# A mixture-of-experts layer whose first 17 expert tiles are formed from three of four images, and the rest from what is left

## The chip, the cores and the metric

One core of one Trainium2 chip. The metric is device time in microseconds (us), the median of the runs shown. Engine names: PE is TensorE (matmul), DVE is VectorE, ACT is ScalarE, POOL is GpSimd, SP is SyncE, which issues DMAs. PEld is TensorE's weight load.

## What is computed

The input is 4 images of 1024 tokens with 256 channels. Three blocks follow one another: a convolution-style attention, a multi-head attention with 8 heads, and a mixture of experts. The change is in the last:

```python
xt = layernorm(t).reshape(-1, 256)                  # 4096 tokens
route_prob = softmax(xt @ Wr + br)                  # 8 experts
routes = argmax(route_prob, axis=-1)
for e in range(8):
    h = gelu(xt @ W1[e] + b1[e])                    # 256 -> 1024
    y = h @ W2[e] + b2[e]                           # 1024 -> 256
    out += y * (routes == e)[:, None]
t = t + out
```

Each token goes to one expert; the kernel computes only that one.

## The kernel before

Work is in blocks of 128 tokens: an image has NB = 8, all four TB = 32. Four phases follow each other, each a block of five instruction streams (one per engine) that ends when all five are done: `conv_phase`, `head_phase`, `output_phase`, `expert_phase`.

`output_phase` (L1136) projects the attention's output, normalises it, and routes it, image by image (b = 0 to 3). VectorE's stream is the loop at L1380: residual and statistics of image b + 1, `positions(b - 1)` (L1364), scale of image b + 1, `router(b)` (L1349); `positions(3)` is behind the loop. `positions(b)` keeps in `prior[:, i, e]` the next free row of expert e before token block i, and turns it into `pos`, the row that each token gets in the scratch table `xs_scr` in DRAM: every expert has a region of 4224 rows there. GpSimd then writes the image's normalised tokens (`lnt`, 257 words each, the last one the token's number) to these rows, eight indirect DMAs of 128 rows (`rows_out`, L1128). Images 0 to 2 are written in the output phase (semaphore `scattered`), image 3 at the start of the expert phase (`last_scattered`).

`expert_phase` (L1394) computes TILES = 39 tiles of 128 rows, each of one expert. 39 is the most that 4096 tokens in 8 experts can need when each expert's last tile is part empty; tiles that are not needed repeat the last one. In the order in which things start:

- SyncE and ScalarE write four blocks of padding each behind the experts' last rows (`pad_rows`, L1455), so that a part-empty tile reads defined rows. Padding rows carry the numbers of spare output rows.
- GpSimd writes image 3's rows.
- VectorE computes the table (L1575 to L1604): tiles per expert, their running sum, then for every tile its expert `texp_i` (semaphore `v_experts`) and its first row `start_i` (`v_start`).
- SyncE waits for all pads, for `last_scattered` and for the table (L1486 to L1488), then loads tile 0's rows (`load`, L1468) and w1 of tile 1 (`weights`, L1473). ScalarE loads w1 of tile 0 once the table is there (L1716 to L1720). The two w1 buffers lie in `lnt` over the blocks 0 to 15.

Then the tiles run. TensorE's stream for tile i (L1684): first layer of tile i + 1 (32 matmuls, `ps_h`), transposes of the tokens of tile i + 2 (`ps_x`), second layer of tile i (16 matmuls, `ps_y`). VectorE (L1636): adds b1 to the first layer of tile i + 1 (`biased`), copies the transposed tokens of tile i + 2 (`xs_c`), adds b2 to the gathered residual rows `t_rows`, and adds the second layer's result (`ys`). ScalarE does the gelu. GpSimd (L1521 to L1561) keeps each tile's token numbers (`take`), scatters `ys` to the output and gathers the next tile's `t_rows`. SyncE loads tokens and w1 of the next tiles; `tokens(i)` (L1480) waits until tile i - 1's were transposed and their numbers taken. Tile 0 and the last two tiles are written out, the rest is a hardware loop of 18 passes over two tiles (`tiles`, L1446, and L1493, L1697). w2 of all experts lies in SBUF.

The table's constants (`TABLE_CONSTS`, L1124) are loaded at the end of the head phase (L893).

Of the kernel before, what the change touches and what calls it, by code (L numbers as in the profile page):

```python
# [24 lines left out]
F32 = mybir.dt.float32  # L25
# [6 lines left out]
P = 128  # L32
# [1091 lines left out]
TABLE_CONSTS = (("expert_no", [P, E]), ("region", [P, E]), ("steps128", [P, TB]), ("tile_no", [P, TILES]))  # L1124
OUTPUT_CONSTS = 8


def rows_out(pool, io, keep, sems, b):  # L1128

    done = sems["last_scattered" if b == B - 1 else "scattered"]  # L1130
    for i in range(b * NB, (b + 1) * NB):
        pool.indirect_dma_start(io["xs_scr"][:, :], bass.IndirectOffsetOnAxis(ap=keep["pos"][:, i:i + 1], axis=0),  # L1132
                                keep["lnt"][:, i, :], None).then_inc(done, 16)


def output_phase(nc, io, keep, sems):  # L1136


    with ExitStack() as ctx:
# [28 lines left out]
        with nc.Block() as block:  # L1168
# [144 lines left out]
            def _(dve):  # L1313
# [65 lines left out]
                scale(0)  # L1379
                for b in range(B):  # L1380
# [13 lines left out]
def expert_phase(nc, io, keep, sems):  # L1394


    with ExitStack() as ctx:
# [11 lines left out]
        expert_no, region, steps128, tile_no = (keep[n] for n, _ in TABLE_CONSTS)  # L1409
        b1_t, b2_all = keep["b1_t"], keep["res0"]  # L1410
        count, ntile, end = sb("count", [P, E]), sb("ntile", [P, E]), sb("end", [P, E])
        base = [sb(f"base{k}", [P, E]) for k in range(2)]
        over = sb("over", [P, E, TB])
        tiled, tiled2 = sb("tiled", [P, TILES, E]), sb("tiled2", [P, TILES, E])
        pad_pos = sb("pad_pos", [P, E], I32)
        start, start_i = sb("start", [P, TILES]), sb("start_i", [P, TILES], I32)
        texp, texp_i = sb("texp", [P, TILES]), sb("texp_i", [P, TILES], I32)
# [19 lines left out]
        v_step, v_pad, v_start = sem("v_step2"), sem("v_pad"), sem("v_start")  # L1437
        w1_in = [sem(f"w1_in{k}") for k in range(2)]
        v_experts, v_xs, v_biased, v_rows, v_ys = sem("v_experts"), sem("v_xs"), sem("v_biased"), sem("v_rows"), sem("v_ys")
# [6 lines left out]
        def tiles(eng, tile):  # L1446

            tile(0, first=True)
            with eng.Fori(0, (TILES - 3) // 2) as p:
                tile(2 * p + 1, parity=1)  # L1450
                tile(2 * p + 2)
            tile(TILES - 2, parity=1, ahead=False)
# [8 lines left out]
        with nc.Block() as block:  # L1461

            @block.sync
            def _(sp):

                pad_rows(sp, range(0, E // 2))
# [19 lines left out]
                sp.wait_ge(padded, 16 * E)  # L1486
                sp.wait_ge(last_scattered, 16 * NB)
# [3 lines left out]
                weights(1, 1, first=True)  # L1491
                tokens(1)
                with sp.Fori(0, (TILES - 3) // 2) as p:  # L1493
                    for k in range(2):
                        tokens(2 * p + 2 + k)
                        weights(2 * p + 2 + k, k)
# [67 lines left out]
            def _(dve):  # L1564
                st = Steps(dve, v_step)

                def step(ins):
                    st.did(ins)
                    st.wait()

                over_e = lambda ap, n: ap.rearrange("p (t o) -> p t o", o=1).to_broadcast([P, n, E])
                over_t = lambda ap, n: ap.rearrange("p (o e) -> p o e", o=1).to_broadcast([P, n, E])
                dve.wait_ge(consts_in, all_consts)

                nc.vector.tensor_copy(pad_pos[:, :], prior[:, TB, :]).then_inc(v_pad, 1)  # L1575

                step(nc.vector.tensor_tensor(count[:, :], prior[:, TB, :], region[:, :], ALU.subtract))
                step(nc.vector.tensor_tensor(over[:, :, :], count[:, :].rearrange("p (e o) -> p e o", o=1).to_broadcast([P, E, TB]),
                                             steps128[:, :].rearrange("p (o t) -> p o t", o=1).to_broadcast([P, E, TB]), ALU.is_gt))
                step(nc.vector.tensor_reduce(ntile[:, :], over[:, :, :], AX.X, ALU.add))  # L1580

                st.did(nc.vector.memset(base[0][:, 0:1], 0.0))
                step(nc.vector.tensor_copy(base[0][:, 1:E], ntile[:, 0:E - 1]))
                c, shift = 0, 1
                while shift < E:
                    st.did(nc.vector.tensor_copy(base[1 - c][:, 0:shift], base[c][:, 0:shift]))
                    step(nc.vector.tensor_tensor(base[1 - c][:, shift:E], base[c][:, shift:E], base[c][:, 0:E - shift], ALU.add))
                    c, shift = 1 - c, 2 * shift
                dve.wait_ge(v_pad, 1)

                step(nc.vector.tensor_tensor(end[:, :], base[c][:, :], ntile[:, :], ALU.add))
                step(nc.vector.tensor_tensor(tiled[:, :, :], over_e(tile_no[:, :], TILES), over_t(end[:, :], TILES), ALU.is_ge))
                step(nc.vector.tensor_reduce(texp[:, :], tiled[:, :, :], AX.X, ALU.add))
                step(nc.vector.tensor_scalar(texp[:, :], texp[:, :], float(E - 1), None, ALU.min))
# [211 lines left out]
```

## Time and profile before

| | us |
|---|---|
| median of three runs | 1250.32 |
| the three runs | 1249.89, 1250.32, 1256.76 |
| span of the profiled execution, first to last instruction | 1249.6 |
| TensorE busy in it | 1141.2 (91%) |
| VectorE, ScalarE, GpSimd busy in it | 665.9, 424.2, 570.6 |

The rows come from one profiled execution, and their times count from its first instruction. A run's time also holds what lies around the span; the median of the runs is 0.7 us above the span, the fastest run 0.3 us. In the rows an engine is busy while one of its instructions runs; registers, semaphores and the issue of DMAs are not counted. "idle before <- x" in a timeline names what ended the wait. The output phase ends at 924.8 us in this execution, the first operation of the expert phase comes at 927.2.

### The profile page before, as it was taken

To read this page: it belongs to the slowest core of one execution; us is meant where nothing else is said; L and a number is where in the kernel's file an instruction comes from. 1 tells how busy PE (TensorE), PEld (TensorE's weight loads), DVE (VectorE), ACT (ScalarE), POOL (GpSimd) and SP (SyncE) were. 2 spreads that over 40 slices of the span, in tenths; PEclk is the share of its full clock that TensorE was granted. 3 is DMA by queue.
4 is the path that set the end of the run, shared out by engine and by line. 5 is a ranking of instruction groups with operands and counts; after the bars stand their busy time and mean duration, and the time that the engine had idled before them with its cause. 6 is when DMAs were issued, how large, how long until landed. Compare 5 with 4: busy or idle time off the path is not lost. (4 is left out here: it accounts for less than half of the span.)

```text
span 1249.6 us, 23166 instructions
## 1 busy us (share of the span) xinstructions
PE 1141.2 (91%) x7476; PEld 811.9 (65%) x7477; DVE 665.9 (53%) x1481; ACT 424.2 (34%) x501; POOL 570.6 (46%) x565
## 2 busy tenths in 40 slices
PE   6899999897679999999999999998726999999995
PEld 3577677575345555555555555556615999999994
DVE  3264636444557777777777777734751333333331
ACT  1302231311115555555555555563520111111110
POOL 0003030110217888888877787860262444444443
PEclk8899999898689999999999999998957999999998
DMA  7204351304151223232232323233445556556551
GB/s 208 60 1 126 129 175 61 126 34 168 68 188 41 94 64 102 71 98 77 76 92 60 93 59 93 60 119 113 160 113 181 192 195 214 189 192 214 194 191 61
DMA packets 61607, 148.42 MB, mean 119 GB/s; under 512 B 11360, under 2 KB 31776, under 8 KB 59904
## 3 DMA queue, kind: packets, MB, share of 16 engines
q1 hardware_dynamic: 53184, 123.39, 31.0%
q0 software_dynamic: 7536, 22.96, 5.7%
q10 hardware_dynamic: 848, 1.58, 0.5%
q8 instruction: 22, 0.36, 0.1%
q14 instruction: 17, 0.14, 0.0%
HBM read 104.58 MB, written 39.87 MB: 116 GB/s over the span
## 5 line engine op out<-in xcount | busy, mean ns | idle before, releaser
L217 DVE TENSOR_REDUCE s_nmax<-ps_v 128x1 f32<-128x512 f32 x484 | 311.5, 685 | 114.5 <-PE ps_v L211 104.6
L923 POOL TENSOR_TENSOR h_added<-h_added,h_expd 128x1024 f32<-128x1024 f32 x124 | 295.5, 2383 | 37.5 <-ACT h_expd L946 29.6
L946 ACT ACTIVATE h_expd<-ps_v 128x1024 f32<-128x1024 f32 x128 | 131.2, 1025 | 154.9 <-PE ps_v L972 150.3
L1669 PEld LDWEIGHTS ps_h<-xs_c,lnt 128*128 128x128 f32 x1248 | 148.0, 195 | 4.8 <-issue 2.9
L1669 PE MATMUL ps_h<-xs_c,lnt 128*128 128x128 f32 x1248 | 148.4, 278 | 2.3 <-DVE xs_c L1621 2.3
L1679 PE MATMUL ps_y<-w,vals_t 128*128 x624 | 141.2, 379 | 0.6 <-DVE ys L1634 0.6
L418 POOL TENSOR_TENSOR a_res<-a_res,a_lnt 128x2048 f32<-128x2048 f32 x4 | 18.2, 4538 | 266.2 <-DVE a_lnt L123 266.2
L986 PE MATMUL h_ps_o<-h_expd,s_vh 128*32 128x256 f32 x2048 | 137.2, 385 | 0.0
L946 ACT ACTIVATE h_expd<-h_ps_e 128x1024 f32<-128x1024 f32 x128 | 130.3, 1018 | 0.0
L580 PE MATMUL a_ps_v<-a_val,a_expd 128*128 128x257 f32 x512 | 123.4, 396 | 5.1 <-ACT a_expd L458 4.5
L1710 ACT ACTIVATE vals_t<-ps_h 128x1024 f32<-128x1024 f32 x39 | 39.9, 1024 | 255.6 <-DVE ps_h L1614 255.6
L1679 PEld LDWEIGHTS ps_y<-w,vals_t 128*128 128x128 f32 x624 | 115.5, 190 | 15.1 <-issue 1.0
L1614 DVE TENSOR_TENSOR ps_h<-ps_h,b_t 128x1024 f32<-128x1024 f32 x39 | 48.1, 1233 | 131.3 <-PE ps_h L1669 131.3
L580 PEld LDWEIGHTS a_ps_v<-a_val,a_expd 128*128 128x128 f32 x512 | 100.4, 198 | 26.0 <-ACT a_expd L458 6.5
L1511 POOL TENSOR_TENSOR pause<-pause 128x1 f32<-128x1 f32 x156 | 30.6, 196 | 156.2 <-DVE ys L1634 131.6
L923 POOL TENSOR_TENSOR h_added<-h_expd 128x1024 f32<-128x1024 f32 x31 | 73.8, 2382 | 55.5 <-ACT h_expd L946 55.5
L986 PEld LDWEIGHTS h_ps_o<-h_expd,s_vh 128*32 128x32 f32 x2048 | 53.6, 109 | 51.9 <-issue 22.4
L689 DVE TENSOR_REDUCE a_nmax<-a_ps_m 128x1 f32<-128x512 f32 x64 | 41.2, 685 | 67.9 <-PE a_ps_m L540 67.9
L608 PE MATMUL a_ps_e<-a_h_c,a_w_qk 128*128 128x512 f32 x128 | 60.3, 624 | 0.3 <-ACT a_h_c L469 0.3
L211 PE MATMUL ps_v<-s_stk2m,s_stk2n 96*128 96x512 f32 x128 | 52.1, 454 | 2.0 <-issue 2.0
L1132 POOL DMA_INDIRECT xs_scr<-lnt,pos x32 | 31.4, 981 | 48.8 <-DVE pos L1373 39.6
L211 PE MATMUL ps_v<-s_stk3m,s_stk3n 96*128 96x512 f32 x128 | 51.4, 447 | 0.0
(208 smaller groups left out, 1530.5 us busy)
## 6 DMA issues: line engine op xcount, KB each, us to landing
lnt<-in_w SPq DMA_DIRECT2D x38, 1024.0 KB, 4.9
qk_scr<-a_head_hi SPq DMA_DIRECT2D x16, 512.0 KB, 2.7
qk_scr<-a_head_lo SPq DMA_DIRECT2D x16, 512.0 KB, 3.6
w<-in_w SPq DMA_DIRECT2D x8, 1024.0 KB, 5.5
xs<-xs_scr SPq DMA_DIRECT2D x39, 128.5 KB, 2.1
a_x_t<-in_x_t POOLq DMA_DIRECT2D x4, 1024.0 KB, 9.8
r_scr<-a_res POOLq DMA_DIRECT2D x4, 1024.0 KB, 5.5
v_scr<-res SPq DMA_DIRECT2D x4, 1024.0 KB, 3.9
```

What stands on the lines that cost most here:

```text
L211: self.nc.tensor.matmul(ps_m[:, half, :], n_st[0:STACK, nb * P:(nb + 1) * P], m_st[0:STACK, half * HALF:(half + 1) * HALF], start=True, st ...
L217: self.nc.vector.tensor_reduce(self.nmax[k][:, nb, half:half + 1], ps_m[:, half, :], AX.X, ALU.max, negate=True).then_inc(self.v_max, 1)
L580: last = nc.tensor.matmul(ps_v[:, j % 2, 0:C + 1], expd[:, m, j * P:(j + 1) * P], val[b % 2][:, m, :], start=(m == 0), stop=(m == NB - 1))
L608: last = nc.tensor.matmul(ps_e[it % 2][:, half, :], w_qk1[:, t, it, :], h_c[:, t, half * HALF:(half + 1) * HALF], start=(t == 0), stop=(t ...
L689: nc.vector.tensor_reduce(nmax[b % 2][:, nb, half:half + 1], ps_m[:, half, :], AX.X, ALU.max, negate=True).then_inc(v_max, 1)
L923: nc.gpsimd.tensor_tensor(total[:, :], (expd[:, 0, :] if m == 1 else total[:, :]), expd[:, m, :], ALU.add).then_inc(g_add, 1)
L946: nc.scalar.activation(expd[:, m, :], flat(ps_e[m % 2]), ACT.Exp, scale=SCALE).then_inc(a_exp, 1)
L986: mm = nc.tensor.matmul(ps_o[j % 2][q * D:(q + 1) * D, 0:QUARTER], vh[j % SLOTS][:, m, :], expd[:, m, q * QUARTER:(q + 1) * QUARTER], star ...
L1614: nc.vector.tensor_tensor(blocks, blocks, b1_t[:, bass.ds(e, 1), :].rearrange("p o (k n) -> p (o k) n", n=1).to_broadcast([P, KC, P]), ALU ...
L1669: last = nc.tensor.matmul(ps_h[k][:, c // 4, c % 4 * P:(c % 4 + 1) * P], w1_now[k][:, t, c * P:(c + 1) * P], xs_c[:, t, :], start=(t == 0) ...
L1679: last = nc.tensor.matmul(ps_y[:, 0:C], hid_t[k][:, c, :], w2[:, bass.ds(e, 1), c, :].rearrange("p o n -> p (o n)"), start=(c == 0), stop= ...
L1710: nc.scalar.activation(hid_t[k].rearrange("p k n -> p (k n)"), flat(ps_h[k]), ACT.Gelu).then_inc(a_gelu, 1)
```

## The change

The tiles come in another order. A first table is made in the output phase, behind `positions(2)` and ahead of `router(3)`, from the counts of three images. It takes only full tiles: 3072 tokens in 8 experts fill at least 17 of them (READY), whatever the routes. These are tiles 0 to 16. The second table is made in the expert phase, in two parts behind tile 0 and tile 1, from the counts of all four images less the tiles already used; it places tiles 17 to 38 and starts each expert behind its used rows. SyncE waits at the phase's start for the scatters of images 0 to 2 and the first table only; the waits for pads, last scatters and second table stand ahead of the load of tile 16. The last image's scatters are issued by GpSimd in three parts behind gather 0, `take(1)` and `take(2)`. The pads are issued behind the first w1 loads. The hardware loops of SyncE, VectorE and TensorE become two, of 7 and 11 passes (VectorE's first has 6, with two tiles written out ahead of it).

```diff
+READY = (B - 1) * NB - (E - 1)
+SCANNED = 1
+class Schedule:
...
+    def stepped(self, dve):
+        def step(ins):
+            self.n += 1
+            ins.then_inc(self.v_step, 1)
+            dve.wait_ge(self.v_step, self.n)
+        return step
+    def tiles_of(self, dve, out, have, keep, full):
+        step, vec = self.stepped(dve), self.nc.vector
+        step(vec.scalar_tensor_tensor(self.count[:, :], have, float(1 - P) if full else 0.0, keep["region"][:, :], ALU.add, ALU.subtract))
+        step(vec.tensor_tensor(self.over[:, :, :], self.count[:, :].rearrange("p (e o) -> p e o", o=1).to_broadcast([P, E, TB]),
+                               keep["steps128"][:, :].rearrange("p (o t) -> p o t", o=1).to_broadcast([P, E, TB]), ALU.is_gt))
+        step(vec.tensor_reduce(out[:, :], self.over[:, :, :], AX.X, ALU.add))
+    def scan(self, dve, ntile):
+        step, vec, base = self.stepped(dve), self.nc.vector, self.base
+        step(vec.memset(base[0][:, 0:1], 0.0))
+        step(vec.tensor_copy(base[0][:, 1:E], ntile[:, 0:E - 1]))
+        c, shift = 0, 1
+        while shift < E:
+            step(vec.tensor_copy(base[1 - c][:, 0:shift], base[c][:, 0:shift]))
+            step(vec.tensor_tensor(base[1 - c][:, shift:E], base[c][:, shift:E], base[c][:, 0:E - shift], ALU.add))
+            c, shift = 1 - c, 2 * shift
+    def place(self, dve, ntile, rows, keep, first, n):
...
+        step(vec.tensor_tensor(end[:, :], base[c][:, :], ntile[:, :], ALU.add))
+        step(vec.tensor_tensor(tiled, over_e(tile_no), over_t(end[:, :]), ALU.is_ge))
+        step(vec.tensor_reduce(texp, tiled, AX.X, ALU.add))
+        step(vec.tensor_scalar(texp, texp, float(E - 1), None, ALU.min))
+        vec.tensor_copy(self.texp_i[:, first:first + n], texp).then_inc(self.v_experts, 1)
+        step(vec.tensor_tensor(tiled, over_e(tile_no), over_t(base[c][:, :]), ALU.subtract))
+        step(vec.tensor_scalar(end[:, :], ntile[:, :], -1.0, 0.0, ALU.add, ALU.max))
+        step(vec.tensor_tensor(tiled2, tiled, over_t(end[:, :]), ALU.min))
+        step(vec.scalar_tensor_tensor(tiled, tiled2, float(P), over_t(rows[:, :]), ALU.mult, ALU.add))
+        step(vec.tensor_tensor(tiled2, over_e(texp), over_t(keep["expert_no"][:, :]), ALU.is_equal))
+        step(vec.tensor_tensor(tiled, tiled, tiled2, ALU.mult))
+        step(vec.tensor_reduce(start, tiled, AX.X, ALU.add))
+        vec.tensor_copy(self.start_i[:, first:first + n], start).then_inc(self.v_start, 1)
+    def early(self, dve, keep, have):
+        self.tiles_of(dve, self.full, have, keep, full=True)
+        self.scan(dve, self.full)
+        self.place(dve, self.full, keep["region"], keep, 0, READY)
+        step, vec = self.stepped(dve), self.nc.vector
+        step(vec.tensor_scalar(self.used[:, :], self.base[SCANNED][:, :], -1.0, float(READY), ALU.mult, ALU.add))
+        step(vec.tensor_scalar(self.used[:, :], self.used[:, :], 0.0, None, ALU.max))
+        step(vec.tensor_tensor(self.used[:, :], self.used[:, :], self.full[:, :], ALU.min))
+    def late(self, dve, keep, have, part):
+        if part:
+            self.place(dve, self.ntile, self.rows, keep, READY, TILES - READY)
+            return
+        self.tiles_of(dve, self.ntile, have, keep, full=False)
+        step, vec = self.stepped(dve), self.nc.vector
+        step(vec.tensor_tensor(self.ntile[:, :], self.ntile[:, :], self.used[:, :], ALU.subtract))
+        step(vec.scalar_tensor_tensor(self.rows[:, :], self.used[:, :], float(P), keep["region"][:, :], ALU.mult, ALU.add))
+        self.scan(dve, self.ntile)
...
-def rows_out(pool, io, keep, sems, b):
+def rows_out(pool, io, keep, sems, b, which=range(NB)):
...
                 scale(0)
+                dve.wait_ge(sems["table_in"], 16 * len(TABLE_CONSTS))
                 for b in range(B):
...
                         positions(b - 1)
+                    if b == B - 1:
+                        keep["schedule"].early(dve, keep, prior[:, b * NB, :])
...
+        PAIRS = (TILES - 3) // 2
+        EARLY_PAIRS = (READY - 3) // 2
...
             def _(sp):
-                pad_rows(sp, range(0, E // 2))
...
+                def loads(first, end):
+                    with sp.Fori(first, end) as p:
+                        for k in range(2):
+                            tokens(2 * p + 2 + k)
+                            weights(2 * p + 2 + k, k)
-                sp.wait_ge(padded, 16 * E)
-                sp.wait_ge(last_scattered, 16 * NB)
+                sp.wait_ge(scattered, 16 * (TB - NB))
                 sp.wait_ge(v_start, 1)
                 load(0)
                 sp.wait_ge(v_experts, 1)
                 weights(1, 1, first=True)
+                pad_rows(sp, range(0, E // 2))
                 tokens(1)
...
+                loads(0, EARLY_PAIRS)
+                sp.wait_ge(padded, 16 * E)
+                sp.wait_ge(last_scattered, 16 * NB)
+                sp.wait_ge(v_start, 2)
+                sp.wait_ge(v_experts, 2)
+                loads(EARLY_PAIRS, PAIRS)
...
             def _(pool):
...
-                rows_out(pool, io, keep, sems, B - 1)
...
                 gather()
+                rows_out(pool, io, keep, sems, B - 1, range(0, 2))
                 take(1)
+                rows_out(pool, io, keep, sems, B - 1, range(2, 5))
                 take(2)
+                rows_out(pool, io, keep, sems, B - 1, range(5, NB))
...
-                tiles(dve, tile)
+                tile(0, first=True)
+                for n in range(2):
+                    schedule.late(dve, keep, prior[:, TB, :], n)
+                    tile(n + 1, parity=1 - n)
+                pairs(dve, tile, 1, EARLY_PAIRS)
+                dve.wait_ge(v_experts, 2)
+                pairs(dve, tile, EARLY_PAIRS, PAIRS)
+                ends(tile)
...
             def _(pe):
...
+                for some in ((0, EARLY_PAIRS), (EARLY_PAIRS, PAIRS)):
+                    if some[0]:
+                        pe.wait_ge(v_experts, 2)
+                    with pe.Fori(*some) as p:
+                        tile(2 * p + 1, parity=1, nth=p + 2)
+                        tile(2 * p + 2, nth=p + 2)
...
             def _(act):
...
-                pad_rows(act, range(E // 2, E))
                 act.wait_ge(scattered, 16 * (TB - NB))
                 act.wait_ge(v_experts, 1)
                 e0 = act.value_load(texp_i[0:1, 0:1], min_val=0, max_val=E - 1)
                 act.dma_start(w1_now[0], io["w1"][bass.ds(e0, 1)].rearrange("o (t p) m -> p (o t) m", p=P)).then_inc(w1_in[0], 16)
+                pad_rows(act, range(E // 2, E))
                 gelu(0, 0, first=True)
```

## Rows read from the trace of the kernel before

**Rows 1.** Stages: PE, PEld, DVE, ACT, POOL busy (x instructions), PEclk, DMA share, GB/s

```profile
924.80:944.80 20.00, 0.00 (x0) 0.00 (x0) 7.15 (x25) 1.28 (x1) 8.05 (x9) 0.50 0.73 165
...
964.20:1225.00 260.80, 260.80 (x1802) 245.93 (x1802) 86.57 (x144) 36.87 (x36) 112.93 (x324) 1.00 0.60 199
```

**Rows 2.** Chain of waits, 905 to 966 us: start us, us, what

```profile
927.90 0.98 POOL xs_scr L1132
...
937.01 6.99 DMA xs_scr<-lnt,pos
...
944.77 2.12 DMA xs<-xs_scr
...
948.39 6.47 PE ps_h L1669 x32
...
956.69 3.81 PE ps_h L1669 x32
```

**Rows 3.** Timeline of VectorE, end of the output phase: start us, us, operation

```profile
913.97 0.17 DVE L1373 CAST pos<-c_pos_f 128x8 int32<-128x8 f32 x1
...
919.46 0.23 DVE L1351 TENSOR_TENSOR c_logits<-c_ps_r,b_rt 128x64 f32<-128x64 f32 x1 [5.32 <-PE c_ps_r L1281]
...
924.62 0.17 DVE L1373 CAST pos<-c_pos_f 128x8 int32<-128x8 f32 x1
...
927.24 0.17 DVE L1575 CAST pad_pos<-prior 128x8 int32<-128x8 f32 x1 [2.45 <-PEq L1168]
```

**Rows 4.** Timeline of VectorE, the table of before

```profile
927.32 0.16 DVE L1577 TENSOR_TENSOR count<-prior,region 128x8 f32<-128x8 f32 x1
...
927.52 0.42 DVE L1578 TENSOR_TENSOR over<-count,steps 128x256 f32<-128x256 f32 x1
...
928.44 0.41 DVE L1583 COPY base<-ntile 128x7 f32<-128x7 f32 x1
...
929.95 0.48 DVE L1592 TENSOR_TENSOR tiled<-tile_no,end 128x312 f32<-128x312 f32 x1
```

**Rows 5.** DMA issues, 928 to 938, then 880 to 924: KB, us to landing

```profile
lnt<-in_w ACTq DMA_DIRECT2D x1, 1024.0 KB, 10.1
...
xs_scr<-padding SPq DMA_DIRECT2D x4, 128.5 KB, 5.6
xs_scr<-lnt,pos POOLq DMA_INDIRECT x8, 7.3
...
xs_scr<-lnt,pos POOLq DMA_INDIRECT x24, 2.6
```

**Rows 6.** Timelines of the sequencers that issue: ScalarE, then SyncE

```profile
928.36 4.36 ACTq L1459 DMA_DIRECT2D xs_scr<-padding  x4
...
945.90 0.41 SPq L1478 DMA_DIRECT2D lnt<-in_w  x1
```

**Rows 7.** Stretches, columns as in rows 1

```profile
931.00:934.00 3.00, 0.00 (x0) 0.00 (x0) 2.79 (x8) 0.00 (x0) 2.39 (x3) 0.50 1.13 221
...
934.00:938.00 4.00, 0.00 (x0) 0.00 (x0) 0.95 (x3) 1.28 (x1) 3.06 (x4) 0.50 1.20 94
...
948.00:950.50 2.50, 2.11 (x10) 2.14 (x11) 0.24 (x1) 0.00 (x0) 1.02 (x1) 0.50 1.03 412
```

**Rows 8.** DMA queues (packets, MB, share) and issues, 980 to 1249 us

```profile
q1 hardware_dynamic: 13957, 39.82, 45.0%
q0 software_dynamic: 3504, 9.57, 10.5%
...
lnt<-in_w SPq DMA_DIRECT2D x33, 1024.0 KB, 4.9
```

**Rows 9.** Timeline of one tile in the loop: VectorE, then TensorE

```profile
967.89 1.23 DVE L1614 TENSOR_TENSOR ps_h<-ps_h,b_t 128x1024 f32<-128x1024 f32 x1 [3.25 <-PE ps_h L1669]
...
969.03 0.41 DVE L1621 COPY xs_c<-ps_x 128x256 f32<-128x256 f32 x1
...
971.26 3.73 PE L1669 MATMUL ps_h<-xs_c,lnt 128*128 128x128 f32 x32
```

More of the change, by code:

```diff
@@ L1125 @@
 OUTPUT_CONSTS = 8
-def rows_out(pool, io, keep, sems, b):
+def rows_out(pool, io, keep, sems, b, which=range(NB)):
     done = sems["last_scattered" if b == B - 1 else "scattered"]
-    for i in range(b * NB, (b + 1) * NB):
+    for i in (b * NB + j for j in which):
         pool.indirect_dma_start(io["xs_scr"][:, :], bass.IndirectOffsetOnAxis(ap=keep["pos"][:, i:i + 1], axis=0),
@@ L1408, in expert_phase @@
         ident = keep["ident"]
-        expert_no, region, steps128, tile_no = (keep[n] for n, _ in TABLE_CONSTS)
         b1_t, b2_all = keep["b1_t"], keep["res0"]
[L1411 to L1414, printed above, removed]
         pad_pos = sb("pad_pos", [P, E], I32)
-        start, start_i = sb("start", [P, TILES]), sb("start_i", [P, TILES], I32)
-        texp, texp_i = sb("texp", [P, TILES]), sb("texp_i", [P, TILES], I32)
+        schedule = keep["schedule"]
+        start_i, texp_i, v_start, v_experts = schedule.start_i, schedule.texp_i, schedule.v_start, schedule.v_experts
         xs, xs_c = sb("xs", [P, C + 1]), sb("xs_c", [P, CT, P])
@@ L1443, in expert_phase, with pairs, ends @@
         all_consts = 16 * len(TABLE_CONSTS)
-        def tiles(eng, tile):
-            tile(0, first=True)
-            with eng.Fori(0, (TILES - 3) // 2) as p:
+        PAIRS = (TILES - 3) // 2
+        EARLY_PAIRS = (READY - 3) // 2
+        def pairs(eng, tile, first, end):
+            with eng.Fori(first, end) as p:
                 tile(2 * p + 1, parity=1)
                 tile(2 * p + 2)
+        def ends(tile):
             tile(TILES - 2, parity=1, ahead=False)
@@ L1577, in _ @@
[L1577 to L1582, printed above, removed]
@@ L1592, in _ @@
-                step(nc.vector.tensor_tensor(tiled[:, :, :], over_e(tile_no[:, :], TILES), over_t(end[:, :], TILES), ALU.is_ge))
-                step(nc.vector.tensor_reduce(texp[:, :], tiled[:, :, :], AX.X, ALU.add))
-                step(nc.vector.tensor_scalar(texp[:, :], texp[:, :], float(E - 1), None, ALU.min))
-                nc.vector.tensor_copy(texp_i[:, :], texp[:, :]).then_inc(v_experts, 1)
-                step(nc.vector.tensor_tensor(tiled[:, :, :], over_e(tile_no[:, :], TILES), over_t(base[c][:, :], TILES), ALU.subtract))
@@ L1603, in _ @@
-                step(nc.vector.tensor_reduce(start[:, :], tiled[:, :, :], AX.X, ALU.add))
-                nc.vector.tensor_copy(start_i[:, :], start[:, :]).then_inc(v_start, 1)
+                nc.vector.tensor_copy(pad_pos[:, :], prior[:, TB, :]).then_inc(v_pad, 1)
+                dve.wait_ge(v_pad, 1)
                 def expert(i):
@@ L1696, in _ @@
                 tile(0, first=True)
-                with pe.Fori(0, (TILES - 3) // 2) as p:
-                    tile(2 * p + 1, parity=1, nth=p + 2)
-                    tile(2 * p + 2, nth=p + 2)
+                for some in ((0, EARLY_PAIRS), (EARLY_PAIRS, PAIRS)):
[4 more added lines that the diff above has]
+                        tile(2 * p + 2, nth=p + 2)
                 tile(TILES - 2, parity=1, nth=TILES // 2 + 1, ahead=False)
@@ L1720, in _ @@
                 act.dma_start(w1_now[0], io["w1"][bass.ds(e0, 1)].rearrange("o (t p) m -> p (o t) m", p=P)).then_inc(w1_in[0], 16)
+                pad_rows(act, range(E // 2, E))
                 gelu(0, 0, first=True)
-                tiles(act, tile)
+                tile(0, first=True)
+                pairs(act, tile, 0, PAIRS)
+                ends(tile)
 def program(nc, io):
```

48 lines of the change are left out of this document (23 added, 25 removed).

## The prediction

> **What bounds the kernel now.** I read the busy time by stages first. Between 924.8 and 944.8 us TensorE does nothing at all; from 964.2 to 1225.0 it is busy every nanosecond at the full granted clock, 260.8 us for 36 tiles, 7.245 us a tile [rows 1]. So inside the tile loop only TensorE counts, and this change leaves its work as it is: 39 tiles, 48 matmuls and two transposes each. What can be won lies in the gap before the loop. The chain of waits says what the gap is made of: eight scatters of the last image issued by GpSimd one after another (927.90 to 937.98, about 1.3 us apart), 6.99 us until the last has landed, 0.77 us on SyncE's sequencer, 2.12 us for the first tile's tokens, then transposes and a copy; the first layer of tile 0 starts at 948.39, that of tile 1 at 956.69 [rows 2]. VectorE's table (7.15 us of busy time from 927.24 on [rows 1, 3]) and the padding stores (issued by 932.7, landed 5.6 us after issue in the middle [rows 5, 6]) end before that last landing, so they are not on the chain. The time forecast below is that start, moved.
>
> **Part 1: the first table moves into the output phase, in front of the last router.** There VectorE ends `positions(2)` at 914.14 and idles 5.32 us until the router's logits at 919.46 [rows 3]. Into this hole goes `early`: 3 operations for the tile counts, 8 for the scan, 13 for the placing, 3 for `used`, each waited for before the next is issued. From start to start a small operation takes 0.20 us (0.16 and a gap of 0.04), the 256-wide one 0.46, a 312-wide one 0.52 [rows 4]; with 17 tiles instead of 39 the wide ones are 136 wide, by a straight line between 8 and 312 wide 0.335 us. Sum: 17 small x 0.20 = 3.4, 2 x 0.46 = 0.9, 8 x 0.335 = 2.7, together 7.0 us. One 7-wide copy of the old table took 0.41 us, where the 8-wide subtraction takes 0.16, and it ended together with GpSimd's first scatter issue (927.90 and 0.98) [rows 2, 4]; image 2's eight scatters run beside `early`, so a few such holds can come: 0 to 0.8 us; I take 0.2. So `early` ends near 921.4, 1.9 us after the logits could be read (bounds 1.3 and 2.6). Router, count and `positions(3)` follow it on the path, so the phase ends 1.9 us later: 926.7 for 924.79, and the first operation behind the block's end comes at 929.1 for 927.24 [rows 3]. What the hole gave, this takes from the gain. The new wait for the constants is met long before.
>
> **Part 2: the first tile no longer waits for the last image.** SyncE and ScalarE now wait at the phase's start for the 24 scatters of images 0 to 2. Scatters of that stretch landed 2.6 us after their issue [rows 5]; the last of image 2 is issued before the old phase ends, so all are in before the new one starts. From the block's end to ScalarE's first DMA took 0.95 us (pads awaited at 927.41, issue at 928.36), and a tile's w1 load follows its token load by 1.13 us on SyncE [rows 2, 6]. So ScalarE issues w1 of tile 0 at 929.95 and SyncE the tokens at about 929.9 (landed 932.0, by rows 2) and w1 of tile 1 at 931.1. What is late next is therefore w1 of tile 0, not the tokens. In the old run it took 10.1 us, behind four pads of its own queue and beside the scatters [rows 5]; in the loop it takes 4.9 [rows 8], and such a load moves at 412 GB/s, 2.55 us for 1.05 MB [rows 7]. Now it is ahead of its pads but shares the engines with w1 of tile 1, issued 1.15 us later: 1.1 us alone (0.45 MB), then 0.6 MB at half rate, 2.9 us. That gives data from 932.1 to 936.1, landed at 936.3. Bounds: 934.9 (not slowed) and 940.0 (10.1 us again). First layer at 936.4: 12.0 us earlier than 948.39.
>
> Here a rule of the Trainium skill can be weighed. The row: loads of the two issuing queues and the scatters were in flight together, and w1 took 10.1 instead of 4.9 us [rows 5, 8]. The Trainium skill, "DMA: Bandwidth & Descriptors", section "Queues, rings and completion order", says that an engine turns from queue to queue packet by packet. By it the two w1 loads share, and the landing is the 936.3 above; were a queue served to its end first it would be 934.9.
>
> **Part 3: what is now put ahead of the second tile.** On SyncE four pads are issued before `tokens(1)`; ScalarE's four took 4.36 us [rows 6], and as many here, with the last wait, put load 1 at about 937.5. Its data stand behind w1 of tile 1 and four pads in SyncE's queue; with ScalarE's four pads and GpSimd's rows 0 and 1 this is ten times 131 KB, 1.3 MB, from 936.1 on. At 412 GB/s they take 3.2 us, at the 221 of the early mixed stretch 5.9, at the 94 of its worst 14 us [rows 7]. I take 221, because the worst stretch had all eight scatters in it and the new one has two: xs(1) lands near 942.6, and first layer 0 (granted clock 0.50, the 1.2 GHz level, after a long idle stretch as before, 6.46 us) ends at 942.9 [rows 2, 7]. Just in time; I book 0.7 us (bounds 0 and 7).
>
> GpSimd issues rows 0 and 1 behind gather 0, rows 2 to 4 behind `take(1)`, rows 5 to 7 behind `take(2)`, at 1.3 us each. By the pattern of the old run GpSimd is then free about when the first `ys` is, near 952.5, and what waits behind it is scatter and gather of the results. On SyncE w1 of tile 2 goes out behind load 2, so it inherits a late xs(1); it needs 4.9 us plus what the scatters take. I book 0.5 us for both (0 to 2).
>
> **Part 4: the second table between the tiles.** `late(0)`: 3 operations, 2 for the rest, 8 of the scan: 11 x 0.20 + 2 x 0.46 = 3.1 us, behind tile 0. `late(1)`: 13 operations, 8 of them 176 wide (0.375): 4.0 us, behind tile 1. VectorE idles 3.25 us there before each bias [rows 9], so the bias of tile 3 comes at most 0.8 us late (1.6 with holds). The next copy `xs_c` starts at 969.03, ends at 969.44, and its first layer begins at 971.26 [rows 9]: 1.8 us of cover. Cost 0; without the cover it would be 0.8. The waits before tile 16 (`padded`, last scatters, second table) stand 14 tiles later, some 100 us after all have ended; nothing queues behind them. The second loop copy on SyncE, VectorE and TensorE: at nothing, with a rival below.
>
> **Sum.** Old start 948.39, new 936.4: 12.0 less 0.7 and 0.5 gives 10.8 us. The profiled span 1249.6 becomes 1238.8. The median of the runs is 0.7 above that span, so the forecast is 1239.5, 0.9% faster. About 1% (12.5 us, below 1237.8) is what a measurement of this kernel can tell from no change, so the likeliest case sits just inside it.
>
> **Rivals.**
> A. *w1 of tile 0 lands unshared and nothing is late behind it*: landing at 934.9, 13.3 us earlier, overrun at its low bound 0.6 less: 13.9, so 1236.4; with one half of the booked losses 1237. For it: 4.9 us in 33 loop loads [rows 8]. Against: a second w1 is issued 1.15 us behind it.
> B. *Pads and scatters jam again*: 94 GB/s between 934 and 938 [rows 7] where pads, scatters and w1 met. If tile 1's tokens (or w1 of tile 0 at 10.1 us) come 3 to 6 us later, the time is 1242.5 to 1245.5. For it: scatters took 7.3 us to land there [rows 5]. Against: six of the eight scatters now come later.
> C. *The doubled tile loops cost on each pass* (the slower end): if the code of a loop no longer stays on the engine, each of the 18 passes pays a fetch. The nearest price is the stretch from the end of one block to the first operation of the next, 924.79 to 927.24, 2.45 us [rows 3]: 18 x 2.45 = 44 us, 1283. It decides from 10.8 / 18 = 0.6 us a pass. Against: from 980 to 1249 us, with the loop of the same length, the queues that moved anything are the two of data alone, none for instructions [rows 8]. The Trainium skill, "Runtime: NRT & Kernel Launch", section "Instruction fetch mechanics", holds that a taken branch out of the two pages held forces a fetch; the trace agrees only in that a loop of this length caused none.
> D. *The gap is held by something else too* (b2, the constants), so nothing is gained: 1250, or 1252 with the overrun. Against: TensorE idled on the tokens alone in the chain [rows 2].
>
> **How the numbers follow.** Forecast 0.61 (own range 1237 to 1242), A 0.16, B 0.18, C 0.03, D 0.02. The range 1236.2 to 1245.5 takes in A, the forecast and B. Faster by over 1%: most of A (0.13) and the low edge of the forecast (0.07), 0.20. Slower by over 1%: C, 0.03. Within 1%: the rest, 0.77.
>
> **What would show it.** Right: VectorE busy without a pause from 914.2 to about 921, the router behind it; first token load near 930; first layer 0 near 936 at half clock; w1 of tile 0 at 6 to 6.5 us to landing; 7.245 us per tile from the third on; no gap of TensorE at tile 16. Wrong: first layer 1 more than 2.5 us behind first layer 0 (step 3), TensorE waiting for `xs_c` or `ys` at tiles 2 to 4 (step 4), instruction packets or a longer period in the loops (C).

## The result and the profile after

| | before | after |
|---|---|---|
| median of nine runs, us | 1254.02 | 1245.35 |
| lowest and highest, us | 1248.88, 1256.76 | 1239.99, 1249.76 |
| ratio to before, 95% interval | | 0.993 (0.9908 to 0.9951) |
| span of the profiled execution, us | 1249.6 | 1247.9 |
| end of image 2's `positions` to the end of the span, us | 335.46 | 327.05 |

The change is worth 0.7%, some 8.7 us of 1254. The forecast was 10.8 us, 0.9%. The two spans differ by only 1.7 us, because the profiled execution of after came to the end of image 2's `positions` 6.7 us later, at 920.85 instead of 914.14, in code that the change doesn't touch: in the stretch 300 to 400 us TensorE was granted 0.74 of its clock there, before it was 0.80 (the late-pads kernel below, with the same code up to there as after, came to that point at 911.69). So all stages below are counted from that point, which I call T ("T + 19.7" is 19.7 us behind it). From T to the end the profiles differ by 335.46 - 327.05 = 8.4 us, near the 8.7 of the nine runs.

The chain of waits of after, where [rows 2] had the scatters (start us, us, what):

```profile
942.21 8.59 DMA xs<-xs_scr
950.85 0.46 PE ps_x L1739 x2
...
953.37 8.81 DMA lnt<-in_w
962.18 0.22 issue
962.41 3.83 PE ps_h L1750 x32
```

The scatters are gone from it. In their place stand two loads: the tokens of tile 1, 8.59 us from issue to landing, and w1 of tile 2, 8.81. TensorE's timeline of after shows what each of them costs (start us, us, operation, idle before and what ended it):

```profile
938.36 0.66 PE L1739 MATMUL ps_x<-ident,xs 128*128 128x128 f32 x2 [8.04 <-DMA xs<-xs_scr]
940.52 5.92 PE L1750 MATMUL ps_h<-xs_c,lnt 128*128 128x128 f32 x32 [1.49 <-DMA lnt<-in_w]
950.85 0.44 PE L1739 MATMUL ps_x<-ident,xs 128*128 128x128 f32 x2 [4.41 <-DMA xs<-xs_scr]
951.89 5.38 PE L1750 MATMUL ps_h<-xs_c,lnt 128*128 128x128 f32 x32 [0.61 <-DVE xs_c L1695]
957.11 0.38 PE L1739 MATMUL ps_x<-ident,xs 128*128 128x128 f32 x2
957.33 3.62 PE L1760 MATMUL ps_y<-w,vals_t 128*128 x16
962.41 3.83 PE L1750 MATMUL ps_h<-xs_c,lnt 128*128 128x128 f32 x32 [1.46 <-DMA lnt<-in_w]
```

First layer 0 starts at 940.52, T + 19.67; before it was 948.39, T + 34.25. That is 14.6 us earlier, more than the 12.0 forecast. Then it is given back: first layer 1 comes 11.4 us behind first layer 0 (before 8.3), first layer 2 comes 10.5 behind that (before 7.3). From first layer 2 to the end both kernels take the same, 285.6 and 285.5 us. The 5.38 us of first layer 1 are TensorE's clock: it had waited 4.41 us with the granted clock still at 1.00, then the clock fell to 0.50, the 1.2 GHz level, as the layer began, and was back at 1.00 from 955.5 on (stretches of after, columns as in rows 1; 0.63 averages the two levels):

```profile
948.00:951.00 3.00, 0.15 (x1) 0.16 (x2) 0.00 (x0) 0.88 (x1) 0.12 (x1) 1.00 0.49 68
951.00:954.00 3.00, 2.39 (x12) 2.18 (x12) 0.42 (x1) 0.00 (x0) 2.36 (x5) 0.63 0.29 69
952.00:952.50 0.50, 0.50 (x3) 0.50 (x4) 0.00 (x0) 0.00 (x0) 0.50 (x1) 0.50 0.00 0
```

The DMA issues of 930 to 946 in after show the traffic in which the tokens stood (KB, us to landing). The four pads of SyncE were issued ahead of the second token load and took 9 us to land:

```profile
lnt<-in_w SPq DMA_DIRECT2D x1, 1024.0 KB, 8.4
xs_scr<-padding ACTq DMA_DIRECT2D x4, 128.5 KB, 8.7
xs_scr<-padding SPq DMA_DIRECT2D x4, 128.5 KB, 9.2
```

**VectorE and the end of the output phase.** VectorE's timeline of after, the lines that answer to [rows 3]:

```profile
920.68 0.17 DVE L1473 CAST pos<-c_pos_f 128x8 int32<-128x8 f32 x1
920.89 0.17 DVE L1165 SCALAR_TENSOR_TENSOR tab_count<-prior,region 128x8 f32<-128x8 f32 x1
...
927.45 0.17 DVE L1212 TENSOR_TENSOR tab_used<-tab_used,tab_full 128x8 f32<-128x8 f32 x1
927.64 0.22 DVE L1451 TENSOR_TENSOR c_logits<-c_ps_r,b_rt 128x64 f32<-128x64 f32 x1
...
932.80 0.17 DVE L1473 CAST pos<-c_pos_f 128x8 int32<-128x8 f32 x1
933.91 0.17 DVE L1677 CAST pad_pos<-prior 128x8 int32<-128x8 f32 x1 [0.93 <-PEq L1268]
```

The first table takes 920.89 to 927.62, 6.7 us; the router runs straight behind it, 1.5 us later than before counted from T (6.79 for 5.32). `positions(3)` ends 1.5 us later too. But the next phase does not: its first operation on VectorE is at T + 13.06, before at T + 13.10. The wait in front of it shrank from 2.45 to 0.93 us. GpSimd's timelines say why, first of before, then of after:

```profile
923.40 0.97 POOL L1132 DMA_INDIRECT xs_scr<-lnt,pos  x1 [0.30 <-issue]
927.20 0.11 POOL L1502 MEMSET pause<- 128x5 f32 x1 [2.84 <-POOLq L1168]
```

```profile
930.06 0.97 POOL L1232 DMA_INDIRECT xs_scr<-lnt,pos  x1 [0.30 <-issue]
933.87 0.11 POOL L1611 MEMSET pause<- 128x5 f32 x1 [2.85 <-POOLq L1268]
```

In both, the new phase begins 2.84 to 2.85 us behind the end of the issue of image 2's last scatter. So GpSimd, not VectorE, seems to end the output phase; experiments below test it. The 924.8 us given ahead of the prediction as that phase's end is only the end of VectorE's work. The row of GpSimd was there to be read; I had read only VectorE's.

### The profile page after: what moved, and what is told of

Its sections match the earlier page's. It is cut to its first block and busy times, and to the rows that moved or that the text cites. A ratio compares the mean times of both kernels' runs of the same rounds, so it can differ in the third digit from the quotient of the medians.

```text
span 1247.9 us, 23191 instructions
## 1 busy us (share of the span) xinstructions
PE 1142.7 (92%) x7476; PEld 812.9 (65%) x7477; DVE 670.7 (54%) x1510; ACT 423.6 (34%) x501; POOL 571.1 (46%) x565
```

## The experiments

Each edit below is to the changed kernel or to the version of it with late pads. The table holds what each trace shows, from T on (FL is the start of a first layer; the columns "0 to 1" and "1 to 2" are the distances between first layers), and the measured ratio to before.

| kernel | new phase | FL 0 | 0 to 1 | 1 to 2 | end | ratio (95%) |
|---|---|---|---|---|---|---|
| before | 13.10 | 34.25 | 8.30 | 7.32 | 335.46 | 1 |
| after | 13.06 | 19.67 | 11.37 | 10.52 | 327.05 | 0.993 (0.9908 to 0.9951) |
| late pads | 13.24 | 19.67 | 8.53 | 7.32 | 321.01 | 0.9875 (0.9858 to 0.9892) |
| late scatters | 13.24 | 19.80 | 10.71 | 9.65 | 325.67 | 0.9907 (0.9887 to 0.9927) |
| both late | 13.40 | 19.73 | 7.10 | 7.32 | 321.23 | 0.9908 (0.9894 to 0.9921) |
| tokens ahead of pads | 12.97 | 19.51 | 7.41 | 10.13 | 322.76 | 0.989 (0.9872 to 0.9909) |
| late pads, table in expert phase | 13.03 | 24.96 | 7.45 | 7.60 | 325.89 | 0.9924 (0.9901 to 0.9947) |
| late pads, w1 of tile 0 early | 15.03 | 19.69 | 8.56 | 7.33 | 321.73 | 0.9888 (0.9864 to 0.9912) |
| late pads, ninth scatter | 14.63 | 20.94 | 7.99 | 9.28 | 323.86 | 0.9891 (0.9868 to 0.9913) |
| pads first | 13.40 | 27.34 | 7.49 | 7.31 | 327.74 | 0.9948 (0.9931 to 0.9965) |
| scatters and pads apart | 13.26 | 19.59 | 7.97 | 7.32 | 322.69 | 0.9905 (0.9877 to 0.9933) |
| late pads, w1 in turn | 13.02 | 19.44 | 7.94 | 7.32 | 320.24 | 0.9888 (0.9861 to 0.9915) |
| late pads again | 13.12 | 19.40 | 7.06 | 7.89 | 320.07 | 0.9885 (0.9857 to 0.9913) |

The intervals are 0.3 to 0.6% wide. The code ahead of T varies from run to run: T lies between 911.69 and 920.85 us in the twelve changed kernels, which do the same work up to there. So the stages within a trace are the finer evidence, each from one execution. One thing in them is chance too: first layer 0 took 5.20 to 6.72 us, as the granted clock rose sooner or later in it, and the column "0 to 1" and the end hold up to 1.5 us of that.

**Which writes hold tile 1.** First the pads alone go later:

```diff
                 weights(1, 1, first=True)
-                pad_rows(sp, range(0, E // 2))
                 tokens(1)
-                loads(0, EARLY_PAIRS)
+                loads(0, 2)
+                pad_rows(sp, range(0, 2))
+                loads(2, 4)
+                pad_rows(sp, range(2, 4))
+                loads(4, EARLY_PAIRS)
...
-                pad_rows(act, range(E // 2, E))
                 gelu(0, 0, first=True)
                 tile(0, first=True)
-                pairs(act, tile, 0, PAIRS)
+                pairs(act, tile, 0, 2)
+                pad_rows(act, range(4, 6))
+                pairs(act, tile, 2, 4)
+                pad_rows(act, range(6, 8))
+                pairs(act, tile, 4, PAIRS)
```

> The eight pads go out two at a time between tiles 4 and 10 instead of ahead of tile 1's tokens; the scatters stay. In the changed kernel first layer 1 starts 11.4 us behind first layer 0, first layer 2 10.5 us behind first layer 1 (8.3 and 7.3 before the change). Theory P, the pads hold tile 1's tokens and the next w1: 8.0 to 8.6 and 7.3 to 8; time 4 to 6 us under the changed kernel, ratio to before about 0.989. Rival S, the last image's scatters do it: 10 or more and 10.5, time within 1 us of the changed kernel.

Measured: 0 to 1 in 8.53, 1 to 2 in 7.32, the end 6.0 us earlier than after, ratio 0.9875. TensorE's timeline of this kernel:

```profile
931.36 6.69 PE L1753 MATMUL ps_h<-xs_c,lnt 128*128 128x128 f32 x32 [1.24 <-DMA lnt<-in_w]
937.88 0.38 PE L1742 MATMUL ps_x<-ident,xs 128*128 128x128 f32 x2
939.89 3.81 PE L1753 MATMUL ps_h<-xs_c,lnt 128*128 128x128 f32 x32 [1.63 <-DVE xs_c L1698]
...
947.21 3.73 PE L1753 MATMUL ps_h<-xs_c,lnt 128*128 128x128 f32 x32
```

No wait for tokens and none for the third w1 (that of tile 2) is left in this trace. Then the scatters alone, and both:

```diff
-                rows_out(pool, io, keep, sems, B - 1, range(0, 2))
                 take(1)
-                rows_out(pool, io, keep, sems, B - 1, range(2, 5))
                 take(2)
-                rows_out(pool, io, keep, sems, B - 1, range(5, NB))
                 pool.wait_ge(t_in, 16)
-                with pool.Fori(0, TILES - 3) as i:
+                for i in range(NB):
+                    results(i)
+                    take(i + 3)
+                    rows_out(pool, io, keep, sems, B - 1, range(i, i + 1))
+                    done(i)
+                with pool.Fori(NB, TILES - 3) as i:
```

> The last image's scatters go out one behind each of the tiles 0 to 7; the pads stay where the change put them. Rival S: first layers 0 to 1 to 2 at 8.0 to 8.6 and 7.3 us, time 4 to 6 us under the changed kernel. Theory P: 0 to 1 stays above 10 us; 1 to 2 falls only if the scatters hold the third w1 load (8.8 us to landing in the changed kernel against 4.9 in the loop), worth at most 3 us.

> Pads and scatters both later. All theories: first layers at 8.0 to 8.6 and 7.25 to 7.4 us, time 5 to 6.5 us under the changed kernel, ratio about 0.988. If P alone is right it equals the kernel with late pads, if S alone it equals the one with late scatters; if it beats both by 1.5 us or more, each does a part.

With the scatters late tile 1's tokens still come late; this is TensorE's timeline with late scatters:

```profile
932.93 6.36 PE L1752 MATMUL ps_h<-xs_c,lnt 128*128 128x128 f32 x32 [1.51 <-DMA lnt<-in_w]
942.34 0.69 PE L1741 MATMUL ps_x<-ident,xs 128*128 128x128 f32 x2 [3.05 <-DMA xs<-xs_scr]
943.64 6.14 PE L1752 MATMUL ps_h<-xs_c,lnt 128*128 128x128 f32 x32 [0.61 <-DVE xs_c L1697]
...
953.29 3.73 PE L1752 MATMUL ps_h<-xs_c,lnt 128*128 128x128 f32 x32
```

The third w1 now lands in time (no wait before 953.29). What is left between 1 and 2 is the clock: first layer 1 takes 6.14 us for 3.81, after 3.05 us of waiting. So the scatters do a small part, the third w1 (1.4 us at the end), the pads the large one. Both late gains nothing on late pads: the two ends are 0.2 us apart, though first layer 0 took 5.25 us there instead of 6.69, which is the clock's chance; it lost 1.6 us in the tiles where its pads went out. Its measured ratio is even 0.3% worse, and the intervals don't meet.

That the third w1 is the scatters' part, not the pads', other traces bear out. In after no DMA moved anything from 950 to 953 us and that load was issued at 953.37, so the pads had landed; with late scatters it landed in 4.8 us; and in the kernel with late pads and a ninth scatter (below), with no pad near, it took 8.60. Views of after, of late scatters (issues of 944.5 to 947) and of the ninth scatter's chain:

```profile
950.00:953.00 3.00, 1.55 (x7) 1.34 (x8) 0.42 (x1) 0.00 (x0) 1.59 (x5) 0.80 0.00 0
```

```profile
lnt<-in_w SPq DMA_DIRECT2D x1, 1024.0 KB, 4.8
```

```profile
946.62 8.60 DMA lnt<-in_w
```

Late pads did not remove this wait for certain, then: it is 0 in the first of its traces, 0.41 us in the second, 1.79 with the ninth scatter. What decides between them is open.

**The order in the queue, or the bytes.** The same bytes, one line moved:

```diff
+                tokens(1)
                 pad_rows(sp, range(0, E // 2))
-                tokens(1)
```

> Only tile 1's token load is moved ahead of SyncE's four pads; the same bytes move. Theory Q, the order in SyncE's queue is what holds tile 1: first layer 1 comes 8.0 to 9 us behind first layer 0, time 2 to 3 us under the changed kernel; the third w1 load stays slow. Rival T, the writes clog all engines whatever the order: 10 us or more, no gain.

```profile
937.65 5.20 PE L1750 MATMUL ps_h<-xs_c,lnt 128*128 128x128 f32 x32 [1.52 <-DMA lnt<-in_w]
944.01 0.44 PE L1739 MATMUL ps_x<-ident,xs 128*128 128x128 f32 x2 [1.16 <-DMA xs<-xs_scr]
945.06 3.81 PE L1750 MATMUL ps_h<-xs_c,lnt 128*128 128x128 f32 x32 [0.61 <-DVE xs_c L1695]
949.34 0.44 PE L1739 MATMUL ps_x<-ident,xs 128*128 128x128 f32 x2 [0.47 <-DMA xs<-xs_scr]
...
955.19 3.83 PE L1750 MATMUL ps_h<-xs_c,lnt 128*128 128x128 f32 x32 [1.18 <-DMA lnt<-in_w]
```

Tile 1 is held by the order for the greater part, as theory Q has it: 0 to 1 falls from 11.4 to 7.4 (0.7 us of it is a shorter first layer 0) and the end by 4.3 us. The issue of the token load here, on SyncE, against 942.21 in after:

```profile
936.87 0.35 SPq L1571 DMA_DIRECT2D xs<-xs_scr  x1
```

The tokens were in 4.1 us earlier, counted from T. Of this 2.6 us are the earlier issue (T + 18.7 for T + 21.4), since SyncE need not issue four pads first, and 1.5 a shorter way (7.1 us to landing for 8.6). In the late-pads kernel they were in at T + 22.6, another 3.3 us earlier: that rest is the pads' traffic. The third w1 stays late (1 to 2 in 10.1), beside the scatters; here some of the pads may still have been in flight too.

**What moving the pads had brought.**

```diff
             def _(sp):
+                pad_rows(sp, range(0, E // 2))
                 sp.wait_ge(scattered, 16 * (TB - NB))
...
-                pad_rows(sp, range(0, E // 2))
                 tokens(1)
...
+                pad_rows(act, range(E // 2, E))
                 act.wait_ge(scattered, 16 * (TB - NB))
...
-                pad_rows(act, range(E // 2, E))
                 gelu(0, 0, first=True)
```

> The changed kernel with the pads where they were before the change: ahead of the first token load and of w1 of tile 0, at the start of the expert phase. Theory P, pads in front of a load cost about their own traffic: w1 of tile 0 takes 8 to 10 us to land and first layer 0 starts at 24 to 26 us behind the end of positions 2 (19.7 in the changed kernel), but first layer 1 follows within 9 us (11.4 there); the end within 2 us of the changed kernel's 327. Rival: w1 is not held by pads that were issued before it: first layer 0 at 22 or earlier and the end 4 us or more under the changed kernel.

The issues of this kernel, 925 to 950: w1 of tile 0 behind the pads lands after 8.1 us, as theory P said.

```profile
lnt<-in_w ACTq DMA_DIRECT2D x1, 1024.0 KB, 8.1
```

First layer 0 comes at T + 27.34, 7.7 us later than in the changed kernel and 1.3 beyond the 26 expected; 5.2 us of that passed before ScalarE issued the load, at T + 19.19 for T + 13.99. The end is 0.7 us later. So putting the pads behind the first w1 loads started the tiles 7.7 us earlier and gave 7 of them back at tile 1 and 2: the pads went from in front of one load to in front of the next.

**Who ends the output phase, and what the early table is worth.** With late pads, the first table back in the expert phase:

```diff
-                    if b == B - 1:
-                        keep["schedule"].early(dve, keep, prior[:, b * NB, :])
...
                 dve.wait_ge(v_pad, 1)
+                schedule.early(dve, keep, prior[:, (B - 1) * NB, :])
```

> Kernel with late pads, and the first table made at the start of the expert phase instead of in the output phase. Times from the end of the third image's positions: there the late-pads kernel has positions 3 done at 12.1, the expert phase's first operation at 13.2, first layer 0 at 19.7, the end at 321.0 us. Theory G, GpSimd's last scatter sets the end of the output phase, so the table there is free: positions 3 at 10.7, first operation still at 13.1 to 13.3, first layer 0 at 26 to 27, the end 6.5 to 7 us later, time 6.5 us over the late-pads kernel. Rival V, VectorE sets it: first operation at 11.6 to 11.8, first layer 0 at 25, the end 5 us later.

VectorE's `positions(3)` ended at T + 9.56 (12.13 with the table there), and the new phase began at T + 13.03 all the same, where rival V had 11.6 to 11.8: theory G. First layer 0 came at T + 24.96 and the end 4.9 us later; these two numbers fit rival V's, but not for its reason. They are less than theory G's 6.5 to 7, because w1 of tile 0 needs only the table's first half, the experts: it was issued at 932.33, the tokens at 934.71, and TensorE no longer waited for it. And with late pads, a ninth scatter (rows that are read nowhere):

```diff
                     rows_out(pool, io, keep, sems, b)
+                pool.indirect_dma_start(io["spare_scr"][:, :], bass.IndirectOffsetOnAxis(ap=keep["pos"][:, (B - 1) * NB - 1:(B - 1) * NB], axis=0),
+                                        lnt[:, (B - 1) * NB - 1, :], None).then_inc(sems["spare"], 16)
```

> Kernel with late pads, and a ninth indirect write of 128 rows behind image 2's eight in the output phase, into a scratch table that nothing reads. Theory G, GpSimd's last scatter issue plus 2.85 us is the end of the output phase: the expert phase's first operation at 14.4 to 14.6 us behind the end of positions 2 (13.2 without), first layer 0 and the end 1.3 us later. Rival V, VectorE: 13.2 as without, no change.

```profile
928.01 0.97 POOL L1293 DMA_INDIRECT spare_scr<-lnt,pos  x1 [0.30 <-issue]
931.83 0.11 POOL L1616 MEMSET pause<- 128x5 f32 x1 [2.85 <-POOLq L1268]
```

Again 2.85 us behind the end of the last issue, and the whole phase 1.4 us later, first layer 0 by 1.3. The end came 2.85 later; the rest lies in 1 to 2 (2.0 more, where the third w1 was late), less 0.5 in 0 to 1.

**Two tries at an earlier w1 of tile 0.** With late pads, ScalarE loads it in the output phase:

```diff
+                schedule = keep["schedule"]
+                act.wait_ge(sems["first_scattered"], 16 * NB)
+                act.wait_ge(schedule.v_experts, 1)
+                e0 = act.value_load(schedule.texp_i[0:1, 0:1], min_val=0, max_val=E - 1)
...
+                act.dma_start(w1_first, io["w1"][bass.ds(e0, 1)].rearrange("o (t p) m -> p (o t) m", p=P)).then_inc(schedule.w1_in[0], 16)
```

> Kernel with late pads, and ScalarE loads w1 of tile 0 at the end of its stream in the output phase, once image 0's scatters are done and the first table has the expert. If the two w1 loads side by side set the start of the first layer (4.9 us in the loop, 5.5 there): w1 is in place before the expert phase, first layer 0 starts at 17.7 to 18.6 us behind the end of positions 2 instead of 19.7 and waits for the tokens; 1 to 2 us under the late-pads kernel, ratio to before about 0.986. If the load only moves its traffic onto the output phase's path or the tokens come no earlier: no gain.

No gain: first layer 0 at T + 19.69 as without. TensorE now waited for the tokens alone, and first layer 0 came 4.7 us behind the start of the phase instead of 6.4, but GpSimd's end of the output phase came later:

```profile
921.97 0.97 POOL L1233 DMA_INDIRECT xs_scr<-lnt,pos  x1 [0.30 <-issue]
927.77 0.11 POOL L1622 MEMSET pause<- 128x5 f32 x1 [4.83 <-POOLq L1269]
```

The wait behind the last scatter grew from 2.78 us (late pads) to 4.83. The scatters took 4.8 us (median) to land beside the w1 load (issues of 916 to 930) where they take 2.5 without it (912 to 925, late pads):

```profile
xs_scr<-lnt,pos POOLq DMA_INDIRECT x6, 4.8
```

```profile
xs_scr<-lnt,pos POOLq DMA_INDIRECT x8, 2.5
```

So the end of the phase follows the landing of GpSimd's last scatter. The other try puts w1 of tile 1 behind tile 1's tokens:

```diff
-                weights(1, 1, first=True)
                 tokens(1)
+                weights(1, 1, first=True)
                 loads(0, 2)
```

> Kernel with late pads, and SyncE issues w1 of tile 1 behind tile 1's tokens, so w1 of tile 0 has the engines to itself. If the two w1 loads share (5.5 us to landing for the first, 6.7 for the second): the first lands 4.9 us after issue, first layer 0 starts at 18.8 to 19.1 us behind the end of positions 2 (19.7 without), first layer 1 still within 8.6 us; 0.6 to 0.9 us faster. If the first load is served to its end whatever is behind it: 19.6 and no change.

The first w1 took 5.4 us to land by itself (925 to 936), and 5.3 with the second beside it (925 to 933, late pads again):

```profile
lnt<-in_w ACTq DMA_DIRECT2D x1, 1024.0 KB, 5.4
```

```profile
lnt<-in_w ACTq DMA_DIRECT2D x1, 1024.0 KB, 5.3
lnt<-in_w SPq DMA_DIRECT2D x1, 1024.0 KB, 6.6
```

The rival holds: the load that is first is not slowed (5.3 to 5.5 us in the seven traces that show it beside the second, with no pads ahead), the second one is (6.6 us). First layer 0 came at T + 19.44, no earlier.

**Pads and scatters apart, and late pads again.** The kernel with late scatters, and pads in ones and twos between tiles 9 and 14:

```diff
-                loads(0, EARLY_PAIRS)
+                loads(0, 4)
+                pad_rows(sp, range(0, 1))
+                loads(4, 5)
+                pad_rows(sp, range(1, 3))
+                loads(5, 6)
+                pad_rows(sp, range(3, 4))
+                loads(6, EARLY_PAIRS)
```

> Scatters of the last image one behind each of the tiles 0 to 7, and the pads in ones and twos between tiles 9 and 14, so that the two kinds of write no longer meet each other nor the first loads. If writes that meet are what delays (the kernel with both late still lost 1.6 us at its pads), first layers at 8.0 to 8.6 and 7.25 us, no TensorE wait at tiles 8 to 14, and 1 us or less from the late-pads kernel, with a lower spread. If any write beside the loop's w1 loads delays, TensorE waits of 0.2 to 1 us show at tiles 9 to 14 and the time is 1 us or more over the late-pads kernel.

The start is undisturbed, but at the pads, behind the last scatter, the loop lost 2.2 us between first layers 12 and 16; TensorE's timeline there:

```profile
1025.63 3.73 PE L1757 MATMUL ps_h<-xs_c,lnt 128*128 128x128 f32 x32
1030.01 0.44 PE L1746 MATMUL ps_x<-ident,xs 128*128 128x128 f32 x2 [0.64 <-DMA xs<-xs_scr]
```

So the two kinds of write need not meet for a loss. Why the pads of the late-pads kernel cost nothing in its loop, in both of its traces (0.5 us with w1 of tile 0 early), is not settled by these runs.

> The late-pads kernel once more, unchanged, beside the two above on the same chip: the end at 321 us behind the end of positions 2, ratio to before 0.986 to 0.990.

0.9885 and T + 320.07: the late-pads kernel is 1.2% faster than before in both measurements, and no kernel here is faster beyond the intervals. From T it beats the change itself by 6 to 7 us, some 0.5%, as the two ratios to before have it too.

## Why the prediction came out as it did

The time, 1245.35, lies just inside the range (1236.2 to 1245.5). Of the 5.9 us between it and the forecast 1239.5, 3.7 are before's own median, which came out at 1254.02 in the nine runs; the gain, 8.7 for 10.8 us, missed by 2.1. Sign and size were about right, but that is in part luck: two steps failed in opposite directions and hid each other.

- **Part 1, the table's own length: right.** 7.0 to 7.2 us expected, 6.7 measured; the router began 1.5 us late, 1.9 expected.
- **Part 1, "so the phase ends 1.9 us later": wrong.** It ended at the same distance from T. The wait of 2.45 us at the block's end in [rows 3] was taken for a fixed cost behind VectorE; it was VectorE waiting for GpSimd, whose last scatter has to land. VectorE had at least 1.5 us of slack that I did not see, and the overrun cost nothing. The ninth scatter and the table's removal from the output phase show it from both sides.
- **Part 2: right in mechanism, w1 mis-sized.** w1 of tile 0 was late next, as said: TensorE waited for it 1.49 us behind the tokens' copy. It was issued at 934.84, 0.93 us behind VectorE's first operation. It took at most 5.7 us to land (the first layer starts at 940.52), where sharing with the second load gave 6.35. The sharing was the error: the first of the two loads takes 5.3 us beside the other and 5.4 alone. By Part 2's estimate, the Trainium skill's rule on turns between queues ("DMA: Bandwidth & Descriptors", "Queues, rings and completion order") would have slowed the first load; the rows here show only the second one slowed. Together with the phase's end, the smaller landing makes the start 14.6 us earlier instead of 12.0.
- **Part 3, "just in time; I book 0.7": the term that failed.** Tile 1's tokens landed 4.4 us behind the end of first layer 0. The bounds of 0 to 7 held it, the choice of 221 GB/s between them did not: the traffic moved at 342 GB/s and then 254 in after, but it was larger than the 1.3 MB I counted, since w1 of tile 1 was still landing, and the last of it trickled (68 GB/s from 948 to 951). Against the sum, the load was issued 2.0 us sooner (T + 21.4 for T + 23.4) and took 3.5 longer (8.6 for 5.1), so the tokens came only 1.5 us later than forecast (T + 30.0 for T + 28.5); the rest of the wait is first layer 0 ending 3.2 us sooner than forecast (T + 25.6 for T + 28.8). The early start of Part 2 ran into it. Of first layer 1's delay 3.1 us are this wait; the clock that fell behind the wait adds 1.6 (5.38 for 3.81), and neither the sum nor the bounds had that term; the third w1, slowed by the scatters, adds 1.5, within the 0 to 2 booked with 0.5. Together 6.2 us with 0.1 of rest, against 1.2 booked.
- **Part 4: right.** From first layer 2 to the end 285.6 us before and 285.5 after; the late tables show no TensorE wait, the second loop none either (rival C): 7.24 to 7.25 us a tile throughout. Two instruction packets moved between 980 and 1249 us, where before had none; they cost no time.
- **The rivals.** B is nearest in the place: tile 1's tokens were late through the pads, and the losses were 5 us over those booked, on top of a start 2.6 us better than the sum. Its jam is not what happened: the traffic moved at 342 and 254 GB/s, not at 94, and with the scatters late TensorE still waited 3.05 us. The greater part is the order of issue on SyncE, which Part 3 had named. A's unshared landing was near too. C and D found nothing for them.
- **The signs.** "First layer 1 more than 2.5 us behind first layer 0" could tell nothing: before has 8.30.

The sum as the runs have it: 14.6 earlier, less 3.1, 1.6 and 1.5, is 8.4 us.

## What to carry to other kernels

When a wait is taken away, look at what the issuing queues now hold in front of the second load, not only the first: here four of the eight pads, which nobody needed for 16 tiles, stood in SyncE's queue in front of tile 1's tokens, and the wait and the clock behind it cost 4.7 of 14.6 us; stores that are due late belong behind the loads that are due soon. When a phase ends for all engines together, find the engine that arrives last before pricing a step on another one; an engine that idles in front of the end has slack to fill. A wait on TensorE can have a price beyond its own length, by the clock in the layer that follows: 1.6 us here, behind 4.41.

## What the runs showed of the hardware that was not expected

- The end of a block with indirect writes on GpSimd came 2.75 to 2.93 us behind the end of the last one's issue in twelve of the traces, and 4.83 in the one where these writes took 4.8 us to land for 2.5. So it follows the landing, not the issue; one trace tells the two apart.
- Waits of 3.05 and 4.41 us on TensorE cost a first layer 2.3 and 1.6 us by the granted clock. It fell from 1.00 to 0.50 within the shorter wait (late scatters, below) and as the layer began behind the longer one (after); waits of 1.6 to 1.8 us in front of a layer cost none.

```profile
941.00:942.00 1.00, 0.00 (x0) 0.00 (x0) 0.00 (x0) 0.73 (x1) 0.00 (x0) 0.85 0.02 8
944.00:945.00 1.00, 1.00 (x6) 1.00 (x6) 0.00 (x0) 0.00 (x0) 0.00 (x0) 0.50 0.15 37
```

- Two loads of 1 MB from two queues, 1.3 us apart: the first landed after 5.3 us, as alone (5.4), the second after 6.6.
- A load of 1 MB beside the last image's indirect writes, with no pads near, took 8.60 us to land with the ninth scatter, 6.9 in late pads again and 5.6 to 5.8 in three other kernels (w1 of tile 0 early, pads first, w1 in turn); with the scatters late it took 4.8 to 5.2.
